# A two-layer graph attention and transformer kernel: loads and a store moved between DMA queues, row sums of x added on GpSimd

## The chip, the cores and the metric

The kernel runs on one core of a Trainium2 chip. The metric is device time in microseconds of one execution, the median of the timed runs. A profiled execution of the same program gives the trace.

## The reference

Two layers are computed on x, eight batches of 512 rows by 512 features, all in float32. Cut to what matters:

```python
# layer 0: graph attention, 16 heads, keys are the first 20 rows, two directions
row_zero = x.sum(-1) == 0
q_exp = where(row_zero[..., None], 0.0, cond[:, None, :])
sf = concatenate([x, q_exp], -1) @ W_self.T + b_self
out = sf
for d in range(2):                      # adjacency and its transpose, 11 labels
    aff = (sf Wq + bq)(kv Wk + bk) / sqrt(32), masked where the labels' sum is 0, + label bias
    out = out + per_head(softmax(aff) @ kv) @ Wout + bout
x = x + relu(out)
# layer 1: transformer attention, 16 heads of 32, 512 keys
h = gamma * layernorm(x) + beta         # gamma, beta from cond
q, k, v = h @ Wqkv.T + bqkv
h1 = (softmax(q k^T) / sqrt(512) @ v) @ Wp.T + bp + x
return gamma * layernorm(h1) + beta + h1
```

The row sums of x are needed for one thing only, the test against zero that keeps or clears the condition's part of `sf`.

## The kernel before, in words

Three stages follow each other, each a block with its own instruction stream per engine; order between engines is kept by semaphores, and each stream's order is written out by hand. The prologue folds weights. The graph stage does layer 0, and the attention stage layer 1. Large products run as three float32r products of high and low parts (`mm3`, lines 107 to 109).

**Graph stage, batches 0 to 7.** Features lie on the partitions: `xraw` holds x of one batch transposed, as four chunks of 128 by 512. ScalarE rounds it to `xh` (`hi_chunk`), GpSimd subtracts to get `xl` (`front`, line 645). Step b works on batch b's scores and on batch b-1's attention:

- TensorE: `self_features(b)` (row sums at lines 1062 and 1063 with a matrix of ones, `mm3` products, and at line 1073 the condition's part, which reads `z`), then `attention(b-1)`, the scores (line 1086) and the transposes back (`back`).
- VectorE: `attention(b-1)`, `label_count(b+1)`, then `softmax(b)`, within it the residual and statistics of batch b-1 (`residual_ln`), then, near the end, `nonzero_rows(b+1)` (line 906), which makes `z` from the row sums; last `labels(b+1)`.
- GpSimd: `front(b+1)`, `label_products(b+1)` (line 650), `lo_rows(b-2)` (line 691), then `softmax(b)` with `back` (`rstd`, line 678) and `add_bp(b-1, i)` (line 685), which adds the projection's bias to `xn`.
- ScalarE: features out of PSUM, rounding of weights and of x for the next batch in turn, exponentials, the normalised rows, and `store_h(b-2)`, a DMA of `xn` to `h_rows` in DRAM.
- SP issues the loads in `step`: x of b+1, labels of b+1 (after VectorE is done with those before, `adj_step`), `xn` anew (after the store of h has landed, `reload_x`), 36 pieces of v, the transposed rows out to `t_rows`, m of b+1. In step 1 eight column loads (`load_columns`, 1024 runs of 4 bytes each) follow m.

The last batch's `xn` is loaded once h of batch 6 is stored; then follow its residual, transposes and q and k products of the next stage.

**Attention stage, batches 0 to 7.** Each batch has four stretches c of four heads, each of 16 slots. A slot of TensorE has one transposed score product (line 1805), one raw score product for the next stretch (line 1818), and three products of q, k, v or output projection (`piece`). ScalarE takes exponentials (line 1565), VectorE row maxima (line 1670). At slot 3 TensorE multiplies the former stretch's key sums (line 1865), at slots 14 and 3 the weighted values (line 1854). q and k are copied into stacks by SP, 12 DMAs per half (`stacks`, line 1313), and a shift row (`sht`) is put under them, its low part by SP (`shift_lo`, line 1319), its high part by ScalarE. The first score product of a half waits for both.

In stretch 1 of batch b the transposed rows of batch b+1 are loaded into `hh` and `hl`: chunks 0 and 1 by ScalarE at slot 9, chunks 2 and 3 by SP, both by a function `load_t` that waits for the batch's last k product. The output of batch b-1 is finished meanwhile, in tiles of 128 rows in two buffers `h[:, i % 2]`: ScalarE loads a tile of h (`load_h`), VectorE adds the projection to it, GpSimd ends it (line 1429), SP stores it (`store_y`, line 1341). `load_h(b-1, 2)` at slot 13 of stretch 1 waits for the store of tile 0, since both use one buffer.

SP's order in stretch 1 before the change (lines 1358 to 1367):

```python
if c < 2 or more:
    stacks(*ahead(b, c, 2), 0, (0,))        # q pieces
if c == 1 and more:
    load_t(b + 1)
if c == 1 and later:
    store_y(b - 1, 0)
if c < 2 or more:
    stacks(*ahead(b, c, 2), 0, (1,))        # k pieces
if c < 3 or more:
    shift_lo(*ahead(b, c, 1), 0)
```

Of the kernel before, what the change touches and what calls it, by code (L numbers as in the profile page):

```python
# [16 lines left out]
F32 = mybir.dt.float32  # L17
# [13 lines left out]
FC = D // P  # L31
# [12 lines left out]
def pieces():  # L44

    out = []
    for g, (k, c) in enumerate(GROUPS):
        row, end = max(k * P, 2 * CK * c), min((k + 1) * P, 2 * CK * (c + 1))
        while row < end:
# [16 lines left out]
                  "stq00 stq01 stq10 stq11 stk00 stk01 stk10 stk11 set_up ones_set bv_done q_ready k_ready qh_done ql_done "  # L66
# [371 lines left out]
def graph(nc, t, d, at):  # L438
# [5 lines left out]
    with ExitStack() as ctx:  # L444
# [34 lines left out]
        s = sems(nc, ctx, "x_in m_in v_in gb_in set_up bits_set pre_done rs_ready z_done adjf_done adjw_done nmr_done sf_ready "  # L479
# [42 lines left out]
        def _(sp):  # L522
# [61 lines left out]
            def step(b, par, last):  # L584
                if not last:
                    sp.wait_ge(s["xl_done"], 4 * b + 4)
                    load_first(b + 1)
                    sp.wait_ge(s["adj_step"], 5 * b + 5)
                    load_adj(b + 1)
# [11 lines left out]
                if isinstance(b, int) and b == 1:  # L601
                    load_columns()
# [20 lines left out]
            stacks(0, 0)  # L623
            reload_x(B - 1)
# [11 lines left out]
        def _(pool):  # L636
# [10 lines left out]

            def label_products(b):
# [4 lines left out]
            def softmax(b, has_former, last=False):  # L653
                for i in range(NT + 2):
# [6 lines left out]
                    if i < 2 and not has_former:  # L661
                        front(b + 1, (2 * i, 2 * i + 1))
                    if i >= 2:
                        pool.wait_ge(s["rc_done"], 4 * b + i - 1)
# [53 lines left out]
            pool.wait_ge(s["hb_done"], 4 * B - 4)  # L718
# [13 lines left out]
        def _(act):  # L732
# [153 lines left out]
            store_h(B - 2)  # L886
# [14 lines left out]
        def _(dve):  # L901
# [141 lines left out]
            nc.vector.tensor_scalar(bcol3[:, 2, :], bcol3[:, 2, :], float(D) ** -0.5, None, ALU.mult).then_inc(la["bv_done"], 1)  # L1043
# [9 lines left out]
        def _(pe):  # L1053
            def self_features(b):
# [6 lines left out]
                for f in range(FC):  # L1061
                    nc.tensor.matmul(bank[:, 1, :], onesr[:, :], xh[:, f, :], start=f == 0, stop=False)
                    last = nc.tensor.matmul(bank[:, 1, :], onesr[:, :], xl[:, f, :],
                                            start=False, stop=f == FC - 1)
# [160 lines left out]
def attention(nc, t, d):  # L1225
# [12 lines left out]
    with ExitStack() as ctx:  # L1238
# [59 lines left out]
        def _(sp):  # L1298
# [818 lines left out]
```

## Time and profile before

| | us |
|---|---|
| median of 3 timed runs | 1318.57 |
| lowest, highest | 1318.37, 1321.41 |
| the profiled execution | 1331.26 |
| its span, first to last instruction | 1329.5 |
| TensorE matmuls busy | 1230.7 (93%) |
| TensorE weight loads busy | 840.6 (63%) |
| VectorE busy | 887.4 (67%) |
| GpSimd busy | 885.6 (67%) |
| ScalarE busy | 633.6 (48%) |
| mean granted TensorE clock | 0.96 of full |

Busy time is the time in which an engine has an instruction running; register, branch, semaphore and DMA-issuing instructions are not counted. In the rows PE is TensorE, PEld its weight load, DVE is VectorE, ACT ScalarE, POOL GpSimd; SPq and ACTq are DMA issues by SP and ScalarE. L1805 is line 1805 of the kernel. A row of the timeline has start, duration, engine, line, operation, written and read tensor, shape, how many such instructions are merged, and in brackets how long the engine was idle before it and what ended that. A row of the groups by line has busy us and mean ns between its bars, then the idle time before the group. A transfer's time to landing is counted from its issue.

### The profile page before, as it was taken

What the parts mean: (1) busy time and instruction counts of PE and PEld (TensorE: products, weight loads), DVE (VectorE), ACT (ScalarE), POOL (GpSimd) and SP (SyncE); (2) the same over time, 40 slices, a digit from 0 to 9 for tenths busy, and PEclk for the clock granted to TensorE, in tenths of its full rate; (3) what the DMA queues carried; (4) which work ended last, traced back from release to release, by engine and by line L of the source; (5) the groups of instructions that cost most, each with busy time, mean ns of one, the idle gap of its engine ahead of it and who ended that gap; (6) DMA issues with size and microseconds to landing.
All of it is one profiled execution on the core that took longest, in us unless ns stands there. A gap on an engine that the chain in (4) does not pass through costs nothing.

```text
span 1329.5 us, 20304 instructions
## 1 busy us (share of the span) xinstructions
PE 1230.7 (93%) x6040; PEld 840.6 (63%) x6040; DVE 887.4 (67%) x1443; ACT 633.6 (48%) x1104; POOL 885.6 (67%) x565
## 2 busy tenths in 40 slices
PE   6989979999999869899999999999999899999985
PEld 4357667777777656566676576576666566666642
DVE  2445758778878755566686686676676677677755
ACT  1323433555355535355365465465465455465551
POOL 1115457677767744676787788788687788788834
PEclk9979989999999979899899999999899999999997
DMA  9883164356435455433433433434524524534411
GB/s 337 318 293 133 33 205 181 124 210 236 149 140 199 152 175 167 112 72 96 144 84 105 140 90 104 143 87 104 145 78 110 147 77 109 147 81 110 112 35 55
DMA packets 106537, 184.11 MB, mean 138 GB/s; under 512 B 38864, under 2 KB 50448, under 8 KB 101184
## 3 DMA queue, kind: packets, MB, share of 16 engines
q1 hardware_dynamic: 96912, 157.80, 38.5%
q10 hardware_dynamic: 9520, 25.06, 6.0%
q8 instruction: 48, 0.79, 0.2%
q14 instruction: 57, 0.47, 0.1%
HBM read 83.92 MB, written 48.01 MB: 99 GB/s over the span
## 4 chain that ended last, share of the span: by engine, by line
PE 50%; DVE 3%; DMA 3%; SPq 2%; issue 2%; ACT 1%; ACTq 0%; POOL 0%; DVEq 0%; POOLq 0%
PE a_bank L1805 9%; PE a_bank L1854 8%; PE a_bank L107 8%; PE a_bank L1818 8%; PE a_bank L108 8%; PE a_bank L109 7%; DMA out_y<-h 2%; PE a_bank L1865 2%; SPq L1313 2%; DVE keep L1670 1%; DVE rden L1688 1%; DMA sq_stack<-sht 1%; ACT pt L1565 1%; PE a_bank L1848 1%; PE a_bank L1829 0%
## 5 line engine op out<-in xcount | busy, mean ns | idle before, releaser
L1670 DVE TENSOR_REDUCE keep<-a_bank 128x1 f32<-128x512 f32 x496 | 333.9, 674 | 232.1 <-PE a_bank L1818 229.5
L1565 ACT ACTIVATE pt<-a_bank 128x512 f32<-128x512 f32 x512 | 303.2, 598 | 377.6 <-PE a_bank L1805 329.5
L1402 POOL TENSOR_TENSOR acc<-acc,pt 128x1024 f32<-128x1024 f32 x120 | 286.7, 2389 | 25.3 <-ACT pt L1565 18.0
L1805 PE MATMUL a_bank<-sq_stack,sk_stack 98*128 98x512 f32 x512 | 222.6, 435 | 23.5 <-ACT pt L1565 11.3
L1818 PE MATMUL a_bank<-sk_stack,sq_stack 96*128 96x512 f32 x496 | 203.2, 410 | 2.9 <-DVE keep L1670 2.2
L1397 POOL TENSOR_TENSOR acc<-pt 128x1024 f32<-128x1024 f32 x60 | 143.5, 2391 | 63.8 <-PE a_bank L1865 48.3
L1805 PEld LDWEIGHTS a_bank<-sq_stack,sk_stack 98*128 98x128 f32 x512 | 99.2, 194 | 115.5 <-issue 80.3
L1086 PE MATMUL g_bank<-m,sf 128*128 128x320 f32 x512 | 140.3, 432 | 1.5 <-ACT g_bank L769 1.5
L1688 DVE RECIPROCAL rden<-a_bank 128x128 f32<-128x128 f32 x128 | 120.5, 944 | 21.0 <-PE a_bank L1848 21.0
L1854 PE MATMUL a_bank<-pt,v 128*32 128x512 f32 x1024 | 124.7, 605 | 0.0
L1086 PEld LDWEIGHTS g_bank<-m,sf 128*128 128x128 f32 x512 | 96.6, 190 | 40.7 <-issue 1.9
L1818 PEld LDWEIGHTS a_bank<-sk_stack,sq_stack 96*128 96x128 f32 x496 | 96.9, 195 | 21.8 <-DVE keep L1670 5.4
L107 PE MATMUL a_bank<-hh,wqkh 128*128 128x512 f32 x240 | 99.6, 415 | 0.0
L108 PE MATMUL a_bank<-hl,wqkh 128*128 128x512 f32 x240 | 99.1, 413 | 0.0
L109 PE MATMUL a_bank<-hh,wqkl 128*128 128x512 f32 x240 | 97.3, 405 | 0.0
L1416 POOL TENSOR_TENSOR ol<-rden,oh 128x512 fp32r<-128x512 f32 x31 | 39.9, 1289 | 59.4 <-ACT rden L1578 59.4
L1854 PEld LDWEIGHTS a_bank<-pt,v 128*32 128x32 f32 x1024 | 27.3, 109 | 63.3 <-issue 62.3
L660 POOL TENSOR_TENSOR e<-e,cadd 128x640 f32<-128x640 f32 x32 | 53.1, 1659 | 19.0 <-DVE e L938 18.9
L645 POOL TENSOR_TENSOR xl<-xraw,xh 128x512 fp32r<-128x512 f32 x28 | 36.5, 1309 | 37.7 <-ACT xh L737 37.7
L962 DVE TENSOR_TENSOR wtl<-g_bank,wth 128x512 fp32r<-128x512 f32 x40 | 27.6, 692 | 47.9 <-ACT wth L785 47.9
L107 PE MATMUL a_bank<-wph,oh 128*128 128x512 f32 x128 | 52.5, 410 | 4.4 <-POOL ol L1416 2.5
L780 ACT ACTIVATE e<-e 128x640 f32<-128x640 f32 x32 | 23.6, 736 | 68.6 <-DVE e L946 68.6
(200 smaller groups left out, 2437.9 us busy)
## 6 DMA issues: line engine op xcount, KB each, us to landing
sq_stack<-qh SPq DMA_DIRECT2D x256, 64.0 KB, 2.0
sk_stack<-kh SPq DMA_DIRECT2D x256, 64.0 KB, 2.1
m<-m_rows SPq DMA_DIRECT2D x8, 1600.0 KB, 8.1
xraw<-in_x_t SPq DMA_DIRECT2D x8, 1024.0 KB, 10.7
xn<-in_x SPq DMA_DIRECT2D x8, 1024.0 KB, 5.4
h_rows<-xn ACTq DMA_DIRECT2D x8, 1024.0 KB, 4.8
t_rows<-houth SPq DMA_DIRECT2D x8, 1024.0 KB, 4.0
t_rows<-houtl SPq DMA_DIRECT2D x8, 1024.0 KB, 6.8
```

The costliest lines, as they stand in the source:

```text
L107: nc.tensor.matmul(out, ah, bh, start=start, stop=False)
L108: nc.tensor.matmul(out, ah, bl, start=False, stop=False)
L109: return nc.tensor.matmul(out, al, bh, start=False, stop=stop)
L1086: last = nc.tensor.matmul(out, sf2[:, par, f, i * P:(i + 1) * P], m[:, f, dr, :], start=False, stop=f == FC - 1, skip_group_check=True)
L1397: nc.gpsimd.tensor_tensor(acc[:, two, :], pt[:, 0, two, :], pt[:, 1, two, :], ALU.add).then_inc(s["sum_done"], 1)
L1402: nc.gpsimd.tensor_tensor(acc[:, two, :], acc[:, two, :], pt[:, step + 1, two, :], ALU.add).then_inc(s["sum_done"], 1)
L1565: nc.scalar.activation(pt[:, i, 2 * half + k, :], bank[:, k, :], ACT.Exp).then_inc(s["exp_done"], 1)
L1670: nc.vector.reduce_max(mx[:, half, k, n:n + 1], bank[:, 2 + e % 2, :], AX).then_inc(s["emax_done"], 1)
L1688: nc.vector.reciprocal(rden[:, c % 2, col], bank[:, KB if final(b, c) and c == 2 else XB, col]).then_inc(s["rden_done"], 1)
L1805: nc.tensor.matmul(bank[:, k, :], sk[c % 2][0:3 * DH + 2, j, i * P:(i + 1) * P], sq[c % 2][0:3 * DH + 2, j, :], start=True, stop=True).the ...
L1818: nc.tensor.matmul(bank[:, 2 + e % 2, :], sq[c % 2][0:3 * DH, j, n * P:(n + 1) * P], sk[c % 2][0:3 * DH, j, :], start=True, stop=True).the ...
L1854: last = nc.tensor.matmul(bank[DH * j:DH * j + DH, OB, :], v[:, vpar, i, (HC * c + j) * DH:(HC * c + j + 1) * DH], pt[:, i, j, :], start=i ...
```

## The change

- The row sums: from batch 1 on GpSimd adds the four chunks of `xraw` into `xs` (a spare buffer), three adds after `front`; TensorE multiplies it with the ones in one float32 product in place of eight float32r ones. SP waits for the adds before it overwrites `xraw`. Batch 0 stays as it was.
- The column loads move from the end of step 1 to behind the x load at its start.
- h of batch 6 is stored by SP behind the first stack pieces, not by ScalarE; the bias adds of that batch stand earlier in GpSimd's last softmax, ahead of the split of wv; GpSimd's memset waits for that split.
- `load_t` is all SP's, in two parts. Part 0 (chunks 0, 1) waits for slot 6 of stretch 1 and stands ahead of the q pieces; part 1 (chunks 2, 3) waits for slot 8 and stands behind the store of y. `load_last` (the last batch's h) is SP's too, behind that store.
- `load_h(b-1, 2)` moves from slot 13 to slot 14. The semaphore `bv_done` goes.

```diff
@@ sync, graph stage
             def step(b, par, last):
                 if not last:
+                    summed = 3 * b if isinstance(b, int) else sp.lower_val(3 * b)
                     sp.wait_ge(s["xl_done"], 4 * b + 4)
+                    sp.wait_ge(s["xs_step"], summed)
                     load_first(b + 1)
+                    if isinstance(b, int) and b == 1:
+                        load_columns()
                     sp.wait_ge(s["adj_step"], 5 * b + 5)
                     load_adj(b + 1)
...
-                if isinstance(b, int) and b == 1:
-                    load_columns()
...
             stacks(0, 0)
+            sp.wait_ge(s["hb_done"], 4 * B - 4)
+            sp.dma_start(d["h_rows"][B - 2], xn[:, :, :]).then_inc(s["h_stored"], 16)
             reload_x(B - 1)
@@ gpsimd, graph stage
+            def row_sums(b):
+                pool.wait_ge(t["x_t_in"], 16 * b + 16)
+                pool.wait_ge(s["rs_ready"], b)
+                for k in range(3):
+                    if k:
+                        pool.wait_ge(s["xs_step"], 3 * b - 3 + k)
+                    nc.gpsimd.tensor_tensor(xs, xs if k else xraw[:, 0, :], xraw[:, k + 1, :], ALU.add
+                                            ).then_inc(s["xs_step"], 1)
...
+                    if i == 1 and not has_former:
+                        pool.wait_ge(t["m_last"], 32)
+                        row_sums(b + 1)
                     if i >= 2:
+                        if last and i in (3, 4):
+                            add_bp(b - 1, i - 3)
...
                 if last:
+                    for i in (2, 3):
+                        add_bp(b - 1, i)
                     split_lo(2)
-                    for i in range(NT):
-                        add_bp(b - 1, i)
...
                     front(b + 1)
+                    row_sums(b + 1)
                     label_products(b + 1)
...
-            pool.wait_ge(s["hb_done"], 4 * B - 4)
+            pool.wait_ge(la["wv_lo"], FC)
@@ scalar, graph stage
-            store_h(B - 2)
@@ tensor, graph stage
+                else:
+                    pe.wait_ge(s["xs_step"], 3 * b)
+                    last = nc.tensor.matmul(bank[:, 1, :], onesr[:, :].bitcast(F32), xs, start=True, stop=True)
@@ sync, attention stage
-            def load_t(b):
-                if not first(b):
-                    sp.wait_ge(s["k_ready"], 4 * b)
-                    sp.wait_ge(s["v_ready"], 4 * b)
+            def load_t(b, part):
+                G = 4 * (b - 1) + 1
+                sp.wait_ge(s["et_ready"], SLOTS * G + 2 * part + 7)
+                two = slice(2 * part, 2 * part + 2)
...
+                    if c == 1 and more:
+                        load_t(b + 1, 0)
                     if c < 2 or more:
                         stacks(*ahead(b, c, 2), 0, (0,))
-                    if c == 1 and more:
-                        load_t(b + 1)
                     if c == 1 and later:
                         store_y(b - 1, 0)
+                    if c == 1 and more:
+                        load_t(b + 1, 1)
+                    elif c == 1:
+                        load_last(b)
@@ scalar, attention stage
-                        if slot == 9 and c == 1:
-                            load_t(b + 1) if more else load_last(b)
                         if later:
-                            if slot == 13 and c == 1:
+                            if slot == 14 and c == 1:
                                 load_h(b - 1, 2)
```

## Rows read from the trace of the kernel before

**Rows 1.** Timeline of TensorE: key sums' products of batches 0 and 6

```profile
530.15 1.04 PE L1865 MATMUL a_bank<-acc,ones 128*32 128x512 f32 x8
...
559.34 1.04 PE L1865 MATMUL a_bank<-acc,ones 128*32 128x512 f32 x8
...
1140.63 1.04 PE L1865 MATMUL a_bank<-acc,ones 128*32 128x512 f32 x8
...
1168.65 1.04 PE L1865 MATMUL a_bank<-acc,ones 128*32 128x512 f32 x8
...
1192.54 1.04 PE L1865 MATMUL a_bank<-acc,ones 128*32 128x512 f32 x8
```

**Rows 2.** Windows: stretch, its length, busy us of the engines, clock, DMA share, GB/s

```profile
632.80:656.80 24.00, 21.56 (x95) 14.94 (x88) 15.46 (x27) 9.55 (x17) 18.69 (x11) 0.90 0.59 176
```

**Rows 3.** Timeline of TensorE, start of stretch 2 in batches 0 and 1

```profile
549.69 0.77 PE L1805 MATMUL a_bank<-sq_stack,sk_stack 98*128 98x512 f32 x1 [2.99 <-issue]
...
652.49 0.77 PE L1805 MATMUL a_bank<-sq_stack,sk_stack 98*128 98x512 f32 x1 [2.44 <-ACT pt L1565]
```

**Rows 4.** Waits: who waited for what, us in total, times, longest us

```profile
ACT pt L1565 <- DMA out_y<-h: 28.0, 5, 7.1
...
DVE xn L974 <- DMA xn<-in_x: 7.3, 1, 7.3
```

**Rows 5.** Timeline of SP's issues, stretch 1 of batch 1

```profile
640.08 1.23 SPq L1313 DMA_DIRECT2D sq_stack<-ql  x2
...
642.59 0.44 SPq L1341 DMA_DIRECT2D out_y<-h  x1
...
647.47 1.23 SPq L1319 DMA_DIRECT2D sq_stack<-sht  x1
```

**Rows 6.** DMA issues from 630 to 660: times, KB each, us to landing

```profile
out_y<-h SPq DMA_DIRECT2D x1, 256.0 KB, 8.7
h<-h_rows ACTq DMA_DIRECT2D x1, 256.0 KB, 3.2
```

**Rows 7.** Timeline of TensorE in the graph stage: row sums, next product, z

```profile
165.36 0.63 PE L1062 MATMUL g_bank<-xh,onesr 128*128 128x512 f32 x1
...
220.73 0.64 PE L1062 MATMUL g_bank<-xh,onesr 128*128 128x512 f32 x1
...
264.74 0.64 PE L1062 MATMUL g_bank<-xh,onesr 128*128 128x512 f32 x1
...
266.84 0.39 PE L107 MATMUL g_bank<-xh,w1h 128*128 128x512 f32 x1
...
275.02 0.84 PE L1073 MATMUL g_bank<-z,sq 128*128 128x512 f32 x3
```

**Rows 8.** Timeline of SP, x load of batch 3

```profile
178.84 0.84 SPq L525 DMA_DIRECT2D xraw<-in_x_t  x1
```

**Rows 9.** Timeline of GpSimd, last operation of the first y tile, batch 1

```profile
639.42 1.29 POOL L1429 TENSOR_TENSOR h<-h,tn 128x512 f32<-128x512 f32 x1
```

**Rows 10.** Waits of SP's queue, label loads

```profile
SPq L528 <- DVE cadd L927: 67.3, 6, 13.3
```

**Rows 11.** Groups by line: score products of the graph stage

```profile
L1086 PE MATMUL g_bank<-m,sf 128*128 128x320 f32 x512 | 140.3, 432 | 1.5 <-ACT g_bank L769 1.5
```

**Rows 12.** Timeline of GpSimd, bias adds of batch 6

```profile
456.50 5.04 POOL L685 TENSOR_TENSOR xn<-xn,bp 128x512 f32<-128x512 f32 x4
```

**Rows 13.** Timeline of GpSimd in step 3: label product and rstd

```profile
246.54 3.65 POOL L650 TENSOR_TENSOR adjw<-adjw,wbias 128x1760 f32<-128x1760 f32 x1 [2.87 <-ACT adjw L775]
...
256.98 1.02 POOL L678 TENSOR_TENSOR rstd<-ve,mhalf 128x4 f32<-128x4 f32 x1 [0.37 <-DVE ve L989]
```

**Rows 14.** Timeline of VectorE, z of batch 4

```profile
273.13 0.74 DVE L906 TENSOR_SCALAR z<-g_bank,hot 64x512 fp32r<-64x512 f32 x1
```

**Rows 15.** Timeline of SP at the end of the graph stage

```profile
455.70 1.22 SPq L581 DMA_DIRECT2D sk_stack<-kl  x2
465.91 0.39 SPq L540 DMA_DIRECT2D xn<-in_x  x1
```

More of the change, by code:

```diff
@@ L65 @@
 ATTENTION_SEMS = ("w_hi w_lo wv_lo wp_hi wp_lo ld_c t_in0 t_in1 h_in0 h_in1 h4_in rows_in "
-                  "stq00 stq01 stq10 stq11 stk00 stk01 stk10 stk11 set_up ones_set bv_done q_ready k_ready qh_done ql_done "
+                  "stq00 stq01 stq10 stq11 stk00 stk01 stk10 stk11 set_up ones_set q_ready k_ready qh_done ql_done "
                   "kh_done kl_done e_ready emax_done sh_ready sh_hi sh_lo shrow_hi shrow_lo et_ready exp_done "
@@ L477, in graph @@
         SFB = (6, 7, 0, 1)
-        s = sems(nc, ctx, "x_in m_in v_in gb_in set_up bits_set pre_done rs_ready z_done adjf_done adjw_done nmr_done sf_ready "
+        xs = t["spare"][:, 0:N]
+        s = sems(nc, ctx, "xs_step x_in m_in v_in gb_in set_up bits_set pre_done rs_ready z_done adjf_done adjw_done nmr_done sf_ready "
                           "sf_done adj_step sc_ready mult_done add_done mx_done sub_done exp_done sum_done "
@@ L1042, in _ @@
             attention(B - 1, 1)
-            nc.vector.tensor_scalar(bcol3[:, 2, :], bcol3[:, 2, :], float(D) ** -0.5, None, ALU.mult).then_inc(la["bv_done"], 1)
+            nc.vector.tensor_scalar(bcol3[:, 2, :], bcol3[:, 2, :], float(D) ** -0.5, None, ALU.mult)
             residual_ln(B - 1)
@@ L1060, in self_features @@
                 pe.wait_ge(s["xl_done"], 4 * b + 4)
[L1061 to L1064, printed above, removed]
+                if isinstance(b, int) and b == 0:
+                    for f in range(FC):
+                        nc.tensor.matmul(bank[:, 1, :], onesr[:, :], xh[:, f, :], start=f == 0, stop=False)
+                        last = nc.tensor.matmul(bank[:, 1, :], onesr[:, :], xl[:, f, :],
+                                                start=False, stop=f == FC - 1)
+                else:
+                    pe.wait_ge(s["xs_step"], 3 * b)
+                    last = nc.tensor.matmul(bank[:, 1, :], onesr[:, :].bitcast(F32), xs, start=True, stop=True)
                 last.then_inc(s["rs_ready"], 1)
@@ L1320, in shift_lo, with load_last @@
                              .rearrange("o k (n c) -> o (k n) c", c=P), sht[:, 1, :].bitcast(F32)).then_inc(s["shrow_lo"], 16)
-            def load_t(b):
-                if not first(b):
-                    sp.wait_ge(s["k_ready"], 4 * b)
-                    sp.wait_ge(s["v_ready"], 4 * b)
+            def load_t(b, part):
+                G = 4 * (b - 1) + 1
+                sp.wait_ge(s["et_ready"], SLOTS * G + 2 * part + 7)
+                two = slice(2 * part, 2 * part + 2)
                 for k, dst in enumerate((hh, hl)):
-                    sp.dma_start(dst[:, 2:4, :].bitcast(F32),
-                                 d["t_rows"][ds(b, 1), k, :, 2:4, :].rearrange("o p c n -> (o p) c n")).then_inc(t_in[1], 16)
+                    sp.dma_start(dst[:, two, :].bitcast(F32),
+                                 d["t_rows"][ds(b, 1), k, :, two, :].rearrange("o p c n -> (o p) c n")).then_inc(t_in[part], 16)
+            def load_last(b):
+                sp.wait_ge(s["pv_done"], 8 * b)
+                sp.dma_start(v[:, 0], d["h_rows"][b]).then_inc(s["h4_in"], 16)
             def load_rows(b):
@@ L1493, in split_hi @@
                 nc.scalar.activation(t["wph"][:, f, :], t["wp_raw"][:, f, :], ACT.Copy).then_inc(s["wp_hi"], 1)
-            def load_t(b):
-                if not first(b):
-                    act.wait_ge(s["k_ready"], 4 * b)
-                    act.wait_ge(s["v_ready"], 4 * b)
-                for k, dst in enumerate((hh, hl)):
-                    act.dma_start(dst[:, 0:2, :].bitcast(F32),
-                                  d["t_rows"][ds(b, 1), k, :, 0:2, :].rearrange("o p c n -> (o p) c n")).then_inc(t_in[0], 16)
             def load_h(b, i):
```

3 lines of the change are left out of this document (removed).

## The prediction

> **What bounds the kernel now.** I read the windows first, then the engines' rows where TensorE is not busy. TensorE is the bound nearly everywhere. In the attention stage its work comes in stretches (a group of four heads) that end with the products of the key sums. From one such group to the next 23.9 us pass where nothing is wrong, but from the one in a batch's second stretch to the one in its third 29.19 us pass in batch 0 and 28.02 us in batch 6 [rows 1]. There are seven such long intervals, one in each of batches 0 to 6 (in order 29.19, 29.34, 28.12, 28.59, 30.33, 29.02, 28.02: 202.6 us); against 7 x 23.89 they hold 35.4 us too much. In batch 1 the window of that place has TensorE busy for 21.56 of 24 us and the granted clock at 0.90 [rows 2]: a stop of 2.44 us, and then products at the lower of the two clock levels, 0.77 us for one [rows 3].
>
> Who stops it: ScalarE's exponentials wait for the store of a result tile (out_y, 28.0 us in five waits; two more of 6.1 and 5.9 us stand under another name at the same place) [rows 4]. Before slot 14 ScalarE loads a tile of h into the buffer that this store empties, so it must wait for it. SP sends the store at 642.59, after the pieces of q (ended 641.31) and two loads of hh and hl [rows 5], and it takes 8.7 us to land, until 651.3, behind four loads of 0.5 MB, two by SP and two by ScalarE [rows 6]. In batch 0 there is no such store, yet TensorE stops for 2.99 us [rows 3]: there the shift row, SP's last issue of the stretch, lands late behind the same four loads. So both causes are at one place, and one is hidden under the other.
>
> In the graph stage a step takes 44.01 us (220.73 to 264.74), but the step before took 55.37 (165.36 to 220.73) [rows 7]. There the x load of batch 3 went out only at 178.84 [rows 8], because eight column loads stand between the load of m and it; ScalarE's rounding of x, and all behind it in its queue, waited. At the end of this stage VectorE waits 7.3 us for the last x [rows 4], and TensorE with it.
>
> **The change part by part.**
>
> *t loads, y store and h load.* The first halves of hh and hl go from ScalarE to SP, behind slot 6 of the second stretch (TensorE, about 636.5 in batch 1). SP sits idle then: the six q pieces wait for slot 7 and take 1.23 / 2 us each, so they start at 637.6 and end at 641.3 as before [rows 5]. The y tile is finished at 640.71 [rows 9], so the store goes out at about 641.4, 1.2 us earlier than 642.59, with two loads of 0.5 MB ahead of it instead of four. A transfer of the same size with little ahead (the h load) lands in 3.2 us [rows 6], so the four loads cost the store 5.5 us, 1.4 each, and two would leave 6.0; but these two are sent some 4 us earlier and are mostly done, so I take 3.2: landed at 644.6 (with 6.0: 647.4; with 8.7: 650.1). ScalarE now asks for it one slot later, near 646, some four us before the next stretch's first product: no wait. The second halves follow the store at 641.9, as now, then the k pieces; the shift row goes at about 647 as before (647.47 [rows 5]) but into a queue with 1 MB less in front. It is due at about 650.0, where TensorE stops now (652.49 less 2.44 [rows 3]). I take 0.7 us as what is left per batch (between 0 and the 2.99 of batch 0). Gain: 35.4 - 7 x 0.7 = 30.5 us, with both stops and the low clock after them gone. In batch 7 the h4 load goes behind the store on SP, and one of ScalarE's five waits (5.6 us in the mean [rows 4]) stands there; TensorE is not full in that batch, so I take 1.5 us (0 to 5.6). What waits behind SP's new waits (q and k pieces, shift row) is issued no later than now. SP's two issues more cost it 0.9 us (0.44 each, as the store's row) in its idle time.
>
> *Column loads.* They move to step 1, behind the x load, ahead of the label load. SP waits there for the labels anyway, up to 13.3 us [rows 10]. The columns keep it for less than the 13.5 us from the start of step 2's row sums (165.36), when m goes out, to the x load, so their price is between nothing and the few us by which the label load lands later; I take nothing. The long step becomes a normal one: 55.37 - 44.01 = 11.4 us.
>
> *Row sums.* Eight float32r products (264.74 to the next work at 266.84: 2.10 us [rows 7]) become one float32 product. The nearest row: the 512 instructions of line 1086 are 256 float32 products of 320 columns, two instructions each, 140.3 / 512 = 0.274 us apiece [rows 11]; at 512 columns that is 2 x 0.274 x 1.6 = 0.88, with the start 1.12 us. Bounds are 0.25 (one product as now) and 2.1. TensorE saves 0.98 us in each of seven steps, 6.9 us. Against it stand three adds on GpSimd, 1.26 us each (5.04 / 4 [rows 12]), 3.8 us per step between the xl splits and the label product. GpSimd is idle for 2.87 us just there and for 0.37 before rstd [rows 13], so rstd comes 3.8 - 2.87 - 0.37 = 0.5 us late, and VectorE waits for it in the middle of its chain. That chain ends in z (273.87), which TensorE reads at 275.02 [rows 14, 7]: 1.15 us to spare, 0.1 of it the semaphore. With TensorE 0.98 earlier and z 0.5 later TensorE waits, and the step is then paced by z: 44.0 - 1.05 + 0.5, a gain of 0.5 per step for the five steps with label products and older rows. In step 0 the adds stand ahead of GpSimd's third softmax add (between 0 and 3.8 us); I take 1.2 us, which eats that step's saving. So 1.0 (step 2) + 5 x 0.5, less 0.3: 3.2 us.
>
> The Trainium skill (SBUF — State Buffer, Who interferes with whom) says that a VectorE instruction with both inputs in SBUF and a GpSimd one that reads SBUF exclude each other. In the gap where the adds go in steps 1 to 6 VectorE reads PSUM or reduces one input, but in step 0 they meet a subtraction of maxima. By the rule one add of 1.26 us could hold it up, and the sum below would be 49.9 instead of 51.2; no row here shows such a pair, and I leave it out.
>
> *End of the graph stage.* GpSimd's four bp adds end at 461.54 behind the split of wv [rows 12]; two now go into its idle places, two ahead of the split, so they end at about 454. SP's first stack pieces end at 456.92 and the x reload was issued at 465.91 [rows 15], 4.4 after the adds: issue and landing of the store. From SP the store goes at 456.9, so the reload at 461.3: 4.6 us earlier, all inside the 7.3 us wait. SP now stands idle for the store's landing, with the second stack pieces behind it; they keep the same distance from the reload. Bounds 0 and 7.3. GpSimd's memset, which now waits for wv's split, comes no later. The dropped bv_done semaphore: nothing waited for it.
>
> **Sum.** 30.5 + 1.5 + 11.4 + 3.2 + 4.6 = 51.2 us off the profiled execution's 1331.3 (span 1329.5 and 1.8 around it): 1280. The timed runs have a median of 1318.6, 12.7 less. Taken off that unchanged the sum gives 1267.4. If the 12.7 lay wholly in the transfers that are waited for here, only 38.5 would be left, 1280. Where it lies no row shows; I take a fifth of it so: **1270 us**.
>
> **Rivals.**
> 1. *The wait goes to VectorE.* The h tile, asked for at about 646.6, lands in 3.2 us [rows 6], at 650, and VectorE adds to it at about 652. If it took the store's 8.7 it would come 3.3 us late, VectorE's maxima behind it, and the clock falls again (2 us more): 6 batches x 5 = 30 us back, 1297 to 1300. For it: the second halves are in flight then. Against it: the row is one of 28 h loads, the seven I read took 3.0 to 3.5 us.
> 2. *The shift row stays late.* In batch 0 it alone stops TensorE for 2.99 us [rows 3]. If half of that is left, 1.5 us, and in every second batch the low clock adds 2 more, 7 x 1.5 + 4 x 2 = 18 us are lost less the 4.9 already in the sum: 1284. The Trainium skill (DMA: Bandwidth & Descriptors, Issuing engines are not separate DMA queues) speaks for it: transfers of all issuing engines share the same 16 DMA engines, so moving a load from ScalarE to SP saves nothing on the way. The trace agrees: the store, on SP's queue, lands late behind loads of both queues. What helps is when they are sent, and the sum uses only that.
> 3. *Columns push elsewhere.* Label load and v pieces of step 1 land late, and the 11.4 us is given back there: 1281.
> 4. *Slower: SP is held by y.* The store now stands ahead of the second halves, k pieces and shift row. If a y tile comes late, each us past 641.5 is one for TensorE. It is worse than before only if it costs over 8.5 us in each of six batches, so y at 650 or later. GpSimd finished it at the same place in all six, 0.6 us ahead of the last q piece [rows 9, 5]. Price at that point: 1320 to 1330.
>
> **Chances.** Forecast 0.66 (own range 1260 to 1280), rival 1 0.10, rival 2 0.12, rival 3 0.06, rival 4 0.02, the remaining 0.04 for something not seen, half of it at no change. A measurement of this kernel tells 0.3% (4 us) from nothing. Faster 0.95, same 0.02, slower 0.03. The range is 1258 (product and stops wholly free) to 1293 (rivals 2 and 3, and rival 1 in part).
>
> **What would show it.** Right: all seven long intervals at 24 to 25.5 us, no ScalarE wait on out_y, out_y landing in 2 to 4 us, granted clock near 1.0 there; step 2 at 43.5 to 44; two PE instructions for the row sum, about 0.9 us; rstd with no idle before it and TensorE waiting some tenths for z; the last x reload near 461 less what was gained before. Wrong: a VectorE wait on h, TensorE waits on the shift row over 2 us, ScalarE waiting for labels in step 1, or a stretch of 29 us that is still there.

## The result, and the profile after

The changed kernel takes 1304.1 us in the median of five runs (1302.6 to 1309.1), the kernel before 1318.5 in the same session: ratio 0.989, interval 0.9865 to 0.9914. A few runs took far longer than the others of their kernel (here one of 3447.7 us, in e5 one of 1591.7, in one session of the kernel before one of 4130.6) and are left out of every time and ratio. 14 us are gained where 48.6 were forecast, and the time lies outside the range. The profiled execution took 1304.1 (span 1302.3).

The timeline of TensorE in the attention stage, key-sum products (L1882, L1865 before) and the first score product of stretch 2 (L1822) in batches 0 and 1:

```profile
515.70 1.04 PE L1882 MATMUL a_bank<-acc,ones 128*32 128x512 f32 x8
...
533.72 0.47 PE L1822 MATMUL a_bank<-sq_stack,sk_stack 98*128 98x512 f32 x1 [0.69 <-issue]
...
540.43 1.04 PE L1882 MATMUL a_bank<-acc,ones 128*32 128x512 f32 x8
...
612.20 1.04 PE L1882 MATMUL a_bank<-acc,ones 128*32 128x512 f32 x8
...
631.79 0.76 PE L1822 MATMUL a_bank<-sq_stack,sk_stack 98*128 98x512 f32 x1 [2.15 <-issue]
...
641.47 1.04 PE L1882 MATMUL a_bank<-acc,ones 128*32 128x512 f32 x8
```

Against [rows 1]: the graph stage ends 14.45 us earlier (530.15 to 515.70). Of the seven long intervals only batch 0's is much shorter (29.19 to 24.73). Batches 1 to 6 still take 29.27, 27.34, 28.06, 26.79, 27.63 and 30.11, 28.20 in the mean after 28.90. Beside a second profile of the kernel before (e1 below) the seven together are only 2.7 us shorter, 193.9 after 196.6. The place of [rows 3] is the same; the name of the wait is not: ScalarE no longer waits for the y store, and TensorE stops for 2.15 us by "issue". The windows of the core (length, busy us of PE, PEld, DVE, ACT, POOL, clock, DMA share, GB/s), of that whole interval and within it:

```profile
612.20:641.47 29.27, 27.12 (x126) 18.19 (x122) 19.02 (x35) 12.39 (x22) 21.57 (x14) 0.88 0.57 154
622.00:629.60 7.60, 7.60 (x40) 4.52 (x39) 5.70 (x13) 3.14 (x6) 7.38 (x6) 1.00 0.94 255
633.00:636.00 3.00, 3.00 (x8) 2.22 (x8) 1.54 (x3) 0.87 (x2) 0.14 (x1) 0.50 0.39 93
```

The DMA engines are full (0.94) in the 7.6 us before the stop, and after it TensorE is granted 0.50, the 1.2 GHz level. SP's issues there:

```profile
616.04 0.33 SPq L1352 DMA_DIRECT2D hh<-t_rows  x1
616.73 0.33 SPq L1352 DMA_DIRECT2D hl<-t_rows  x1
617.22 3.63 SPq L1337 DMA_DIRECT2D sq_stack<-qh  x4
620.89 1.22 SPq L1337 DMA_DIRECT2D sq_stack<-ql  x2
622.16 0.58 SPq L1370 DMA_DIRECT2D out_y<-h  x1
622.78 0.46 SPq L1352 DMA_DIRECT2D hh<-t_rows  x1
623.28 0.45 SPq L1352 DMA_DIRECT2D hl<-t_rows  x1
623.83 2.42 SPq L1337 DMA_DIRECT2D sk_stack<-kh  x4
626.30 1.23 SPq L1337 DMA_DIRECT2D sk_stack<-kl  x2
627.57 0.68 SPq L1343 DMA_DIRECT2D sq_stack<-sht  x1
```

And the landing times of that place (DMA issues from 616 to 634: times, KB each, median us to landing), beside [rows 6]:

```profile
sk_stack<-kh SPq DMA_DIRECT2D x7, 64.0 KB, 5.1
...
out_y<-h SPq DMA_DIRECT2D x1, 256.0 KB, 2.5
h<-h_rows ACTq DMA_DIRECT2D x1, 256.0 KB, 5.6
sk_stack<-kl SPq DMA_DIRECT2D x2, 64.0 KB, 4.8
```

The y store lands in 2.5 us instead of 8.7, as predicted. What follows it is late: the k pieces take 5 us to land, the h load 5.6 instead of 3.2. Between 622 and 629.6 1920 KB are asked for (y 256, t 1024, k 384, h 256), at 255 GB/s 7.7 us of work, and what was sent last lands last.

In the graph stage (PE, POOL, VectorE; step 4's row sum, then step 4's and 5's GpSimd work):

```profile
253.17 1.02 PE L1088 MATMUL g_bank<-spare,onesr 128*128 128x512 f32 x2
...
275.05 1.30 POOL L650 TENSOR_TENSOR xl<-xraw,xh 128x512 fp32r<-128x512 f32 x1 [0.53 <-ACT xh L758]
276.31 1.29 POOL L660 TENSOR_TENSOR spare<-xraw 128x512 f32<-128x512 f32 x1
277.68 2.64 POOL L660 TENSOR_TENSOR spare<-spare,xraw 128x512 f32<-128x512 f32 x2
280.27 3.65 POOL L665 TENSOR_TENSOR adjw<-adjw,wbias 128x1760 f32<-128x1760 f32 x1
...
288.79 1.55 POOL L675 TENSOR_TENSOR e<-e,cadd 128x640 f32<-128x640 f32 x1
288.81 1.56 DVE L1006 TENSOR_SCALAR ve<-mv 128x3 f32<-128x3 f32 x1
290.72 1.02 POOL L698 TENSOR_TENSOR rstd<-ve,mhalf 128x4 f32<-128x4 f32 x1 [0.38 <-DVE ve L1009]
```

The long step is gone (164.87 to 208.44: 43.57 us after 55.37), but each of the four steps that follow takes 44.7 to 44.8 instead of 44.01.

### The profile page after: what moved, and what is told of

Read it like the earlier page. It is cut to its first block, busy times and chain, and to the rows that moved or that the text cites. A ratio compares the mean times of both kernels' runs of the same rounds, so it can differ in the third digit from the quotient of the medians.

```text
span 1302.3 us, 20256 instructions
## 1 busy us (share of the span) xinstructions
PE 1215.0 (93%) x5998; PEld 820.2 (63%) x5998; DVE 891.2 (68%) x1443; ACT 634.1 (49%) x1104; POOL 914.4 (70%) x586
## 4 chain that ended last, share of the span: by engine, by line
PE 67%; DVE 7%; POOL 6%; issue 6%; SPq 2%; DMA 2%; ACT 2%; ACTq 0%; DVEq 0%; POOLq 0%
PE a_bank L1822 10%; PE a_bank L1835 9%; PE a_bank L1871 9%; PE a_bank L107 9%; PE a_bank L108 9%; PE a_bank L109 8%; PE g_bank L1110 4%; PE a_bank L1882 2%; SPq L582 2%; PE g_bank L107 2%; PE g_bank L109 1%; PE g_bank L108 1%; POOL e L675 1%; POOL xl L650 1%; POOL xn L705 1%
## 5 line engine op out<-in xcount | busy, mean ns | idle before, releaser
L1822 PE MATMUL a_bank<-sq_stack,sk_stack 98*128 98x512 f32 x512 | 221.3, 432 | 19.7 <-issue 14.6
L1822 PEld LDWEIGHTS a_bank<-sq_stack,sk_stack 98*128 98x128 f32 x512 | 98.3, 192 | 111.4 <-issue 77.5
L1458 POOL TENSOR_TENSOR tn<-tn,rows 128x512 f32<-128x512 f32 x28 | 36.1, 1288 | 32.0 <-ACT tn L1605 32.0
L108 PEld LDWEIGHTS a_bank<-hl,wqkh 128*128 128x128 f32 x240 | 47.8, 199 | 11.3
```

The costliest lines, as they stand in the source:

```text
L108: nc.tensor.matmul(out, ah, bl, start=False, stop=False)
L1822: nc.tensor.matmul(bank[:, k, :], sk[c % 2][0:3 * DH + 2, j, i * P:(i + 1) * P], sq[c % 2][0:3 * DH + 2, j, :], start=True, stop=True).the ...
```

## The experiments

Before's level moved by some us between sessions, so ratios are to before's runs of the same session. The long intervals in one view (from the timelines; us):

| kernel | batch 0 | mean of 1 to 6 | batch 7 | time | ratio, interval |
|---|---|---|---|---|---|
| before | 29.19 | 28.90 | 22.49 | 1318.5 | |
| before, second profile (e1) | 27.42 | 28.19 | 22.49 | 1320.2 | |
| after | 24.73 | 28.20 | 23.47 | 1304.1 | 0.989 (0.9865 to 0.9914) |
| e2 no row sums | 24.31 | 28.13 | 23.21 | 1302.8 | 0.985 (0.9817 to 0.9883) |
| e3 only t loads | 23.82 | 28.13 | 23.38 | 1318.0 | 0.9956 (0.9931 to 0.9981) |
| e5 shift row first | 26.74 | 25.55 | 23.80 | 1295.2 | 0.9786 (0.9755 to 0.9818) |
| e6 second half last | 23.46 | 25.67 | 23.31 | 1292.4 | 0.9766 (0.9734 to 0.9797) |
| e7 h late | 23.96 | 25.65 | 24.78 | 1297.3 | 0.9797 (0.9749 to 0.9844) |
| e8 t early, row, k | 24.50 | 27.39 | 23.79 | 1300.9 | 0.982 (0.9791 to 0.9848) |
| e9 t early, k, row | 24.42 | 26.20 | 23.47 | 1290.4 | 0.9743 (0.9701 to 0.9784) |
| e10 adds ahead of splits | 26.14 | 27.69 | 22.98 | 1294.4 | 0.9793 (0.9752 to 0.9835) |
| e11 t second half 1/8 | 22.45 | 24.00 | 22.82 | 1281.2 | 0.969 (0.9647 to 0.9732) |
| e12 h load 1/8 | 26.05 | 25.21 | 22.93 | 1288.7 | 0.9743 (0.9703 to 0.9782) |
| e13 t second half by ScalarE | 22.89 | 24.42 | 23.52 | 1280.0 | 0.9659 (0.9624 to 0.9695) |
| e14 e13 and e10 | 23.33 | 24.14 | 23.41 | 1278.6 | 0.9641 (0.9611 to 0.967) |

The kernel after, e2 and e10 have the same order in the attention stage, and their means of batches 1 to 6 are 28.20, 28.13 and 27.69; before's two traces have 28.90 and 28.19. So a difference of 0.7 us in such a mean tells nothing. Batch 0 varies by up to 1.8 us between kernels that do not differ there.

**e1, before once more.**

> The kernel before, unchanged, for a second profile. The question is where the 12.7 us lie by which its first profiled execution stood above its timed runs, and so what they would have taken from each term of the sum. Theory A: that execution had slower transfers, so the places that wait for transfers are shorter here: the seven long attention intervals sum to about 190 to 195 us instead of 202.6, and step 2 of the graph stage stays near 55. Theory B: the 12.7 us are spread or lie where no transfer is waited for (a later start, the tail), and the seven intervals again sum to 200 to 205. Theory C: the profile itself adds them, and the second profiled execution also stands 10 us or more above the timed ones.

1320.2 us with its profile, no more than the timed runs of its session (1318.1 to 1333.3), so the profile adds nothing (not C). Theory A, in part. This execution is 11.0 us shorter than the first profiled one. The seven intervals sum to 196.6 instead of 202.6. Step 2 of the graph stage takes 53.46 instead of 55.37, of which 0.9 is left at the first key sums (529.23 after 530.15). From the last key sums to the end it takes 63.2 instead of 66.2. So 6.9 of the 11.0 us lie in places that the sum had counted at full price. The same place looks otherwise from run to run. In batch 0 TensorE stops for 4.33 us here and for 2.99 in [rows 3], and yet the interval is the shorter one:

```profile
548.43 0.47 PE L1805 MATMUL a_bank<-sq_stack,sk_stack 98*128 98x512 f32 x1 [4.33 <-issue]
...
549.06 0.63 PE L107 MATMUL a_bank<-hh,wqkh 128*128 128x512 f32 x1
```

The low clock follows here too, but for less time: 0.70 is granted in the 5 us from 549.23, against 0.50 and then 0.90 in the 10 us from 550.15 before. In the first profile the clock was also low ahead of the stop (0.74 from 540.15 to 545.15, here 1.00), so TensorE came to slot 0 later and had less to wait.

**e2, row sums taken back.** All edits of the row sums undone in the kernel after.

```diff
# TensorE
-                if isinstance(b, int) and b == 0:
-                    for f in range(FC):
...
-                else:
-                    pe.wait_ge(s["xs_step"], 3 * b)
-                    last = nc.tensor.matmul(bank[:, 1, :], onesr[:, :].bitcast(F32), xs, start=True, stop=True)
+                for f in range(FC):
...
# GpSimd
-                    row_sums(b + 1)
```

> The kernel after with its row sums taken back: TensorE's eight float32r products in every step, no adds on GpSimd. Theory A (row sums cost time: GpSimd's three adds take 3.9 us where it was idle for 2.87, and all behind them comes 1.05 us late; TensorE's saving is worth only 0.3): the steady graph step falls from 44.75 to 44.0 us, the first key-sum group comes 2.5 to 4 us earlier than 515.7, and the time falls by 3 to 4 us from 1304.8 to about 1301. Rival (the prediction's): row sums gain 3.2 us, so this kernel is that much slower, 1308. Rival 2: the step is 44.75 us for another reason (ScalarE's store of h waits for GpSimd either way), and the step stays at 44.7.

0.985 (0.9817 to 0.9883) against after's 0.989 (0.9865 to 0.9914): the intervals of the times overlap, so the traces decide. They have steps of 44.0 again and the first key sums at 510.85 (after 515.70): 4.9 us. The row sums cost time, and the rivals fall.

**e3, e4, e15: one part of the change alone on the kernel before.** e3: t loads, y store, h and h4 loads. e4: the column loads. e15: the end of the graph stage.

> The kernel before with only the attention stage's edits: both halves of the t load on SP, the first ahead of the q pieces, the second behind the y store, h asked for in slot 14, h4 load on SP. Theory A (the shift row, SP's last issue, lands late behind 1 MB of t and takes back most): only batch 0's interval becomes normal, the others lose less than a us each, 4 to 10 us in all: 1309 to 1314. Rival (as predicted): 30 us, 1287. Rival 2: these edits give nothing and what was gained came from the graph stage alone: 1318.

> The kernel before with only the eight column loads moved, from behind the m load to behind the x load of step 1. As predicted: step 2 of the graph stage takes 44 instead of 55.4 us, the first key-sum group comes 11.4 us earlier, and the time falls by 11.4 to about 1307. Rival A: the timed runs hold a shorter step 2 than the profiled one (a part of the 12.7 us between them), and only 5 to 8 us are gained: 1311 to 1313. Rival B: what is gained is taken back at the end of the graph stage by the last x, less than 4 us are left.

> The kernel before with only the edits at the end of the graph stage: bias adds of batch 6 two earlier in the last softmax and two ahead of the split of wv, store of h by SP. As predicted: the reload of x 4.6 us earlier and the time 4.6 lower, 1314. Rival: the first key-sum group comes 5 us earlier in the kernel after because of the columns and not of this; here 0 to 1 us, 1318. Rival 2: up to 7 us, the whole wait for the last x.

e3: 0.9956, 5.8 us. In its trace batch 0 is 3.6 to 5.4 us shorter than in before's two; the other six are at 28.13 in the mean, where before's are at 28.19 and 28.90. e4: 0.992 (0.9892 to 0.9948), 10.5 us; steps of 44.0 from step 2 on. e15: 0.9943 (0.9921 to 0.9965), 7.5 us (4.6 to 10.4). Its profiled run, slower than its median, has the store by SP and the reload at 460.30, 4.3 us before e1's 464.63 and 5.6 before [rows 15]:

```profile
456.17 0.58 SPq L625 DMA_DIRECT2D h_rows<-xn  x1
460.30 0.40 SPq L540 DMA_DIRECT2D xn<-in_x  x1
```

The parts, 10.5 + 7.5 + 5.8 less 5.3 for the row sums (0.4%, e2), make 18.5; measured are 14.5 of before's 1318.5, and the intervals of the parts overlap that.

**e5 to e7: what is late in stretch 2.** From here on, edits to the kernel after.

```diff
# e5, SP, c == 1
+    shift_lo(*ahead(b, c, 1), 0)
     stacks(*ahead(b, c, 2), 0, (1,))
-    shift_lo(*ahead(b, c, 1), 0)
# e6, SP, c == 1
-    load_t(b + 1, 1)
     stacks(*ahead(b, c, 2), 0, (1,))
     shift_lo(*ahead(b, c, 1), 0)
+    load_t(b + 1, 1)
# e7, ScalarE
-    if slot == 14 and c == 1:
+    if slot == 0 and c == 2:
         load_h(b - 1, 2)
```

> The kernel after with one exchange in stretch 1 of every batch: SP sends the low part of the shift row ahead of the six k pieces (which are for the group after next) instead of behind them. In the kernel after the row's data are there at 624.9 in batch 1 and it is issued at 627.57, due at 629.6, and TensorE stops until 631.8. Theory A (the row is late, behind the second halves of t and the k pieces on the same DMA engines): it is issued 2.6 us earlier with 384 KB less in front and lands 1.5 to 2.6 us earlier; the six long intervals fall from 28.2 in the mean to 24.5 to 26.5, 10 to 20 us in all: 1286 to 1295. Theory B (pieces of q or k of an earlier stretch, or something that is not the row, ends the wait): the intervals stay at 28: 1305. Theory C (the h load of ScalarE takes the transfer time): unchanged or 1 us per batch, 1299 to 1305.

> The kernel after with the second half of the t load (1 MB) sent behind the shift row instead of ahead of the k pieces. Theory A (the row waits for that 1 MB): the row is issued at about 626.6 in batch 1 with nothing large before it, the stop at the first score product of stretch 2 goes, the intervals fall to 24 to 25, over 20 us in all: 1280 to 1285. The halves are then due at about 632.6 and sent at 627.3; if they land late, TensorE stops one or two slots later, at the products of hh's third chunk, and half of the gain is lost: 1292. Theory B (something else ends the wait): the intervals stay at 28, 1305. Theory C (h load): as B, a little less.

> The kernel after with the third h load of each batch (256 KB, ScalarE) asked for at slot 0 of stretch 2 instead of slot 14 of stretch 1, so that it doesn't share the DMA engines with the shift row. Theory C (this load, new at this place, is what keeps the row late; batch 0, which has neither y store nor h load, is cured): the stop goes, intervals 24 to 25: 1281. Theory A (1 MB of t and the k pieces do it): 256 KB less is worth up to 0.9 us per batch, 0 to 5 us: 1300 to 1305.

All three give 2.5 us per batch, and in each TensorE then stops for what was now sent last. In e5 it is the raw score product (L1837), for the pieces of k, first in batch 1, then in batch 3; in e6 the product that reads the third chunk of hh:

```profile
633.30 0.47 PE L1837 MATMUL a_bank<-sk_stack,sq_stack 96*128 96x512 f32 x1 [1.90 <-issue]
...
827.87 0.50 PE L1837 MATMUL a_bank<-sk_stack,sq_stack 96*128 96x512 f32 x1 [1.20 <-DMA sk_stack<-kl]
```

```profile
828.68 0.58 PE L107 MATMUL a_bank<-hh,wqkh 128*128 128x512 f32 x1 [2.68 <-DMA hl<-t_rows]
```

In e7 the row is still 0.5 to 1.6 us late in three batches, the k pieces 0.5 to 0.6 in two others, and VectorE now waits for h and TensorE for what VectorE makes behind it (0.4 to 1.2 us, 2.7 in batch 7). So theory A names a true cause, but not the only one: I had taken the k pieces, for the group after next, as not urgent. The raw scores run one group ahead of the transposed ones, and shift row, k pieces and two slots later t are due together. Theory B's "not the row" is true of e5. Theory C fell short of curing it, but 256 KB are worth more than the 0.9 us that A gave them.

**e8 and e9: t as early as its buffers allow.**

```diff
# SP, c == 1; e8 puts shift_lo ahead of the k pieces, e9 leaves it behind them
     load_t(b + 1, 0)
+    load_t(b + 1, 1)
     stacks(*ahead(b, c, 2), 0, (0,))
     store_y(b - 1, 0)
-    load_t(b + 1, 1)
     stacks(*ahead(b, c, 2), 0, (1,))
```

> The kernel after with both halves of t sent as soon as their buffers are free (slots 6 and 8), ahead of the q pieces, then q pieces, y store, shift row, and the k pieces last. Theory A (transfer time ahead of the row is the cause, and when it is sent decides): no large transfer is sent after 619 in batch 1, the row lands near 627, intervals at 23.9 to 24.5, the granted clock at 1.0: 27 to 29 us in all, 1276 to 1280. Theory B: 28 us stay, 1305. A rival that loses: the q pieces, sent 1 us later and behind 2 MB, hold up the overwriting of qh or the y store, and a new stop of 2 us stands in stretch 2: 1290.

> As the run with t sent early, but with the k pieces ahead of the shift row again (order on SP: t halves at slots 6 and 8, q pieces, y store, k pieces, shift row). That run showed TensorE stop for 1.1 to 2.8 us at the raw score product, which needs the k pieces of the group after, not at the transposed one, which needs the shift row: both are due in slot 0 of stretch 2. Theory A (everything that SP sends in stretch 1 is due in slot 0, and with t out of the way it is SP's issuing that is last): k pieces end at about 627.3 and the row at 628 in batch 1, land by 630; stops of 0 to 0.7 us, intervals 24 to 25, 1283 to 1287. Theory B (the sum of bytes up to slot 0 decides, whatever their order): stops of 2 us as in the kernel after, intervals near 27, 1297 to 1301.

e8 missed by 20 us: SP waits there for the row's data (12.7 us after the key sums) with the k pieces behind it, done at 17.2 to 17.9, where both are due at 17.4. e9 leaves 1 to 1.8 us of stop; the row goes at 15.7 to 17.2. Batch 1 of e9, SP and then TensorE:

```profile
629.97 0.68 SPq L1343 DMA_DIRECT2D sq_stack<-sht  x1
```

```profile
632.67 0.47 PE L1821 MATMUL a_bank<-sq_stack,sk_stack 98*128 98x512 f32 x1 [1.18 <-issue]
```

The first product that needs the row starts 2.0 to 2.7 us after the row's issue in batches 1 to 6, against 4.2 to 5.0 in the kernel after. Now it is the issue that is late. SP's rows ahead of it in batch 1, the second half of t for hh and the q pieces:

```profile
620.23 0.33 SPq L1352 DMA_DIRECT2D hh<-t_rows  x1
...
621.14 2.80 SPq L1337 DMA_DIRECT2D sq_stack<-qh  x4
```

**e11 and e12: the price of two loads.**

```diff
# e11, SP: n = P // 8 for the second half; e12, ScalarE: n = P // 8 for i == 2
-    dma_start(dst[:, ...], src[:, ...])
+    dma_start(dst[0:n, ...], src[0:n, ...])
```

> The kernel after, but of the second half of each t load only 16 of 128 partitions are loaded (128 KB instead of 1 MB), so what is computed of the later batches is not the reference's; the order of all issues is kept. It prices these 896 KB. Theory A (they are what keeps shift row and k pieces late): all seven intervals at 24 to 24.5, TensorE's stops under 0.3 us: 1278 to 1282. Theory C (the h load is the cause): intervals 26 to 27, at most half of the gain: 1293.

> The kernel after, but of the h load in slot 14 only 16 of 128 partitions are loaded (32 KB instead of 256), so the outputs of these rows are not the reference's; the order of all issues is kept. It prices this load without sending it at another time. Moved to stretch 2 it gave 15 us back, where 256 KB at 300 GB/s are 0.9 us a batch. Theory C (it stands in the way of the row by more than its bytes, being on another queue that takes turns with SP's): stops fall to 0.5 us or less and intervals to 24.5 to 25.5, 1286 to 1292. Theory A (only bytes count): 0.9 us less a batch and at most the low clock after it: intervals 26 to 27.5, 1293 to 1300.

In both a part of the data is left out, so they price a load and are no version to use. Without 896 KB of t all is cured: 24.00 us, in batches 1 to 6 no stop at slot 0. Without 224 KB of h the six intervals fall by 3.0 us each. The stops at slot 0 went from about 2.1 us in the mean (1.3 to 2.9) to 0.8: 1.3 us, where 224 KB at 255 GB/s are 0.9. The other 1.7 are products at the low clock, which no longer follow: in the 10 us from 17 us after the key sums on, the kernel after is granted 0.66 to 0.83 in five of the six batches, e12 1.00 in all six. Interval (25.2) and time (1288.7) are those of theory C, but its reason is not borne out: the stop fell by little more than the bytes, and the clock doubled that. Theory A counted the bytes rightly and the clock too low.

**e13, SP's issuing.**

```diff
# SP: load_t(b + 1, 1) gone; ScalarE:
+    if slot == 9 and c == 1 and more:
+        load_t1(b + 1)      # hh, hl [:, 2:4], after et_ready of slot 8
```

> The kernel after with the second half of the t load issued by ScalarE in slot 9 of stretch 1 instead of by SP behind the y store; SP's order is first halves, q pieces, y store, k pieces, shift row. The same bytes as in the run with t early, sent nearly as early, but SP's queue is two issues shorter ahead of the pieces. Theory D (with t out of the way SP's issuing sets when the shift row goes: 9.5 us of issues from slot 7 on, row at 15.9 after the key sums there and due at 17.4): the row goes 1 us or more earlier, at 14.5 to 15, and the intervals fall from 25.9 in the mean to 24 to 24.6: 1280 to 1284. Theory E (the bytes are too many for the time in any order): intervals near 26 again, 1290. The kernel before had ScalarE send halves at this place too, but also the store behind them, on which ScalarE waited.

Batch 1, SP's issues, the two of ScalarE, and TensorE's first product of stretch 2:

```profile
614.74 2.44 SPq L1337 DMA_DIRECT2D sq_stack<-qh  x4
617.23 1.22 SPq L1337 DMA_DIRECT2D sq_stack<-ql  x2
618.50 0.59 SPq L1370 DMA_DIRECT2D out_y<-h  x1
619.18 2.73 SPq L1337 DMA_DIRECT2D sk_stack<-kh  x4
621.95 1.31 SPq L1337 DMA_DIRECT2D sk_stack<-kl  x2
623.30 0.68 SPq L1343 DMA_DIRECT2D sq_stack<-sht  x1
```

```profile
617.04 0.33 ACTq L1530 DMA_DIRECT2D hh<-t_rows  x1
617.41 0.53 ACTq L1530 DMA_DIRECT2D hl<-t_rows  x1
```

```profile
627.56 0.47 PE L1829 MATMUL a_bank<-sq_stack,sk_stack 98*128 98x512 f32 x1 [0.45 <-issue]
```

The row goes 13.6 us after the key sums (609.67), with the bytes of e9; 24.42 in the mean, 1280.0 us. Theory D holds, E falls. But the two issues are only a part of it. In batch 1 of e9 the row goes at 15.9 (629.97, key sums at 614.05), 2.3 us later. The q pieces start 2.0 us later there, at 7.1 against 5.1: SP first stands until slot 8 for the second half (sent at 6.2), 1.2 us, and then issues it, 0.8 us. No run takes the wait and the issuing apart.

**e10 and e14, GpSimd's adds ahead of its splits; and all together.**

```diff
-    front(b + 1)
     row_sums(b + 1)
+    front(b + 1)
     label_products(b + 1)
```

> The kernel after with GpSimd's three adds ahead of its four xl splits in each step (from the gap where it waits for ScalarE's xh) instead of behind them. Theory A (the adds cost time because they end 1.05 us after the point where GpSimd used to wait for ScalarE's adjw): splits and adds together end at about the old time, the label product starts when adjw is there, the steady graph step falls from 44.75 to 43.7 to 44.0, five steps, 4 to 5 us: 1300. Theory B (the adds cost time by what they take from VectorE or from ScalarE's store of h): the step stays at 44.7: 1305.

> The same with GpSimd's three adds ahead of its xl splits (e10). The two are in different stages and should add: e10 stood about 5 us below the kernel after by its step of 43.7 us, so this one 4 to 6 us below e13: 1275 to 1279 by theory D, 1285 by theory E.

In e10 GpSimd waits 2.87 us for the label again and rstd starts 35.7 us after the step's row sum (253.08 to 288.80; 37.6 in the kernel after); steps of 43.7, and 0.9793 (0.9752 to 0.9835):

```profile
266.33 1.28 POOL L660 TENSOR_TENSOR spare<-xraw 128x512 f32<-128x512 f32 x1
267.69 2.64 POOL L660 TENSOR_TENSOR spare<-spare,xraw 128x512 f32<-128x512 f32 x2
270.28 5.19 POOL L650 TENSOR_TENSOR xl<-xraw,xh 128x512 fp32r<-128x512 f32 x4
278.34 3.65 POOL L665 TENSOR_TENSOR adjw<-adjw,wbias 128x1760 f32<-128x1760 f32 x1 [2.87 <-ACT adjw L796]
```

So theory A holds, and in this order the row sums no longer cost time. That they gain any is not shown: a later step takes 43.7 us where it takes 44.0 without them (e2), but the first key sums come at 511.44, not ahead of e2's 510.85. The time, 1294.4, fell by 10 us where 4 or 5 were expected. In the profiled executions 4.3 us are gained up to the first key sums and 2.3 behind them, where nothing was changed. e14 has the lowest time: 1278.6, by the ratios 2.5% under the kernel after. Over e13 it brings 1.3 us, which the intervals of the two do not tell from nothing, though its first key sums are 3.1 us earlier (511.93, 515.05). In its profiled execution batch 0 takes most of that back: the interval after the long one is 26.33 us instead of e13's 23.63. There the products run at the low clock after a stop of 0.45 us, the clock of that window being 0.77 (1.00 in e13):

```profile
545.00:560.00 15.00, 14.74 (x60) 9.73 (x64) 7.15 (x13) 8.09 (x14) 10.79 (x6) 0.77 0.23 54
```

## Why the prediction was wrong, step by step

1. *t loads, y store, h load: 30.5 us forecast, 5.8 came (e3).* The first half was right: the store lands in 2.5 us (forecast 3.2), and ScalarE's wait is gone. The step that failed is "I take 0.7 us as what is left per batch". It gave the shift row "a queue with 1 MB less in front", as if the halves sent early were done and nothing else were in the way. But the DMA engines stay full up to the stop (0.94). The same 2 MB of t, the pieces of q and k, y and now h too must pass before slot 0, the second halves were still sent ahead of k pieces and row, and the row was issued at 14.9 us after the key sums (mean of batches 1 to 6) instead of 15.5. Left were 28.20 - 23.89 = 4.3 us per batch, not 0.7: 3.6 too much in each of six, 21.7 us. Batch 0, without y and h, came out at the number forecast (24.6, measured 24.73), but by luck: TensorE has less to do there, and with little late it takes 22.5 to 22.9 us (e11, e13) and not the 23.89 that was taken for all seven. That both causes sat at one place was said; that the second had as large a price as the first was not drawn from it, though [rows 3] showed it: with no store to wait for, 2.99 us of stop and a 29.19 us interval.
2. *Batch 7: 1.5 us gained forecast, 1.0 lost* (22.49 to 23.47). TensorE now stops for 0.75 us at the first score product of stretch 2, where it did not before. SP sends the 1 MB load of h4 there, behind the store of y and ahead of k pieces and row; that this is the cause was not tested.
3. *Columns: 11.4 forecast, 10.5 (e4); 11.4 in the trace of e4 (a step of 44.02 after 55.37).* Right, though in e1 the long step itself is only 53.46.
4. *Row sums: 3.2 gained forecast, 5 lost (e2).* The product is near the forecast (two instructions, 1.02 us where 1.12 with the start was reckoned), and GpSimd ends the adds 1.05 late (3.92 from 276.31 against an idle 2.87). What failed is "the step is then paced by z". ScalarE's store of h waits for GpSimd's last bias add either way (ACTq at z + 5.32 us in both kernels), so TensorE's saving ends there, 0.3 us being left; and the slack of "0.37 before rstd" was not one: that idle remains 0.38 and moves with the rest. 1.05 - 0.3 = 0.75 us per step; measured are 0.74, in four steps. Of the rest of the 4.9 us about 0.4 lies in the earlier steps (step 0 is 1.7 us longer than in e2, steps 1 and 2 together 1.3 shorter), and where the remainder arises no run shows.
5. *End of the graph stage: 4.6 forecast; the reload 4.3 to 5.6 earlier (e15).* Right.
6. *The 12.7 us.* A fifth was taken off; of the 11.0 that e1 has less, 6.9 lay in the counted places.

Rival 2 named the mechanism, and the rule of the Trainium skill that it cites holds: bytes of all queues share the DMA engines (in e12 224 KB less on ScalarE's queue took 1.3 us off the stop for what SP sends). It was priced from half of batch 0's stop, without y store and h load, and came out at 1284. The Trainium skill (DMA: Bandwidth & Descriptors, Issuing engines are not separate DMA queues) goes on that starting transfers on several engines saves only issuing time, usually small against the transfer. Here it was not small: from e9 to e13 the bytes are the same, two issues of SP's went to ScalarE, and 10.4 us were gained. A part of that is SP's wait ahead of the two issues, which held up everything behind it. Rivals 1, 3 and 4 did not occur.

## What to carry to other kernels

When a wait is removed, list everything else that is due at the same slot, with its bytes, and divide by the rate of that window: if the DMA engines are full until then, another order changes which transfer is last and gains only a part (2.5 of 4.3 us per batch in e5 to e7). Send large transfers as soon as the buffer is free, and count the time of the issuing engine too, its waits included, for all that stands behind them. An engine's idle time is free for new work only up to the wait that follows; work put ahead of an idle that something else ends costs little or nothing (e10), behind it its overrun passes through the whole step.

## What the runs showed of the hardware

- A stop of TensorE costs more than its length, but not always. In the kernel after, 2.15 us in batch 1 were followed by products of 0.63 us (granted 0.50), and the interval was 5.4 us over 23.89. In batch 4 the longer stop of 2.65 us was followed by products at full speed (0.40 us, granted 1.00), and the interval was 2.9 us over:

```profile
933.22 0.47 PE L1822 MATMUL a_bank<-sq_stack,sk_stack 98*128 98x512 f32 x1 [2.65 <-issue]
```

- Four q pieces took SP 3.63 us in batch 1 of the kernel after and 2.44 in e13, at the same place behind the same two loads of t. No run shows why.
- VectorE's small operation on ve (L1006) took 1.56 us when it started 0.02 behind GpSimd's add at 288.79, and ended with it. In e10 it started in the middle of the same add and took 0.51, again up to the add's end; the shortest of its eight in the kernel after took 0.17. By the Trainium skill (SBUF — State Buffer, Who interferes with whom) a VectorE operation with a scalar can take both port pairs, one of which is GpSimd's, and then waits for the whole of a GpSimd instruction that came first: the trace agrees. It is not what the step lost: in the kernel before the operation took 0.50 us and ended with the add too, and in all three kernels rstd starts 0.38 us behind the end of that add.
